# Receptance product moved ahead of the value product and the numerator scan in an RWKV block's time mix, on eight cores

## The chip, the cores and the metric

The kernel runs on all 8 cores of one Trainium2 chip, each core with one of the 8 sequences of the batch and its own copy of all weights. The cores exchange nothing. The metric is the device time in microseconds (us) of the slowest core; lower is better.

## The reference, cut to what matters

One RWKV layer (time mix, then channel mix) with a residual and a layer norm around it, then a feed-forward layer with dequantized weights and again a residual and a layer norm. Each core has 4096 rows of 1024 values. The change lies in the time mix:

```python
xn = _ln(x, ln1_g, ln1_b)
xp = _shift(xn)
k = (xn * mix_k + xp * (1.0 - mix_k)) @ Wk
v = (xn * mix_v + xp * (1.0 - mix_v)) @ Wv
r = jax.nn.sigmoid((xn * mix_r + xp * (1.0 - mix_r)) @ Wr)
# _wkv, over the positions t:
#   ek = exp(k_t);  a = ew * a + ek * v_t;  b = ew * b + ek
#   out_t = a / (b + 1e-8)
wkv = _wkv(k, v, time_decay, time_first)
x = x + r * wkv @ Wo
```

The two recurrences have one decay `ew` for each feature. The quotient is computed as `a * exp(-ln(b + 1e-8))`.

## The kernel before, in words

A core works through its rows in 8 blocks of 512 positions (h = 0 to 7). The Python code records all instructions once, in program order, with the buffers that each reads and writes; every engine then runs its own instructions in that order, and a semaphore wait is put in wherever another engine (or the same one, where a result is needed at once) must be done first. Nothing is reordered, so the order in which the code records is the order of the work. Buffers are tracked by name: `T1` and `T2` are one name each, though they hold 8 slices of 512 columns, while the 32 slices of `bigbf` have a name each (`bg0` to `bg31`).

For a block the stages are: load and first layer norm (`stage_pre`), transposes (`stage_tr1`), the mixes (`stage_mix_k`, and `stage_mix_vr`, which makes all 8 slices for v and then all 8 for r on VectorE), `stage_attn`, the channel mix (`stage_fA`), the middle norm, the feed-forward (`stage_fB`), and the last norm (`stage_tail`). `stage_pre` of the next block is recorded inside `stage_fA`, `stage_mix_k` inside `stage_fB`. `stage_mix_vr` and `stage_attn` stand alone between one block's tail and its own `stage_fA`.

`stage_attn` has these parts, each over 8 output slices `mo` of 128 features; a product of one slice is 8 matmuls of 512 columns into one PSUM bank (`kvr_mm`, L614):

1. k loop: k product, then ScalarE takes the exponential into `T1` (L633).
2. v loop: v product into the four banks psA, psB, psO0, psO1 in turn; VectorE multiplies it with `T1` into `sc_ekv` (L651); ScalarE writes the decay into one of two halves of `ew_t` (L657); VectorE scans the numerator (L662), copies the carry (L668), scans the denominator (L673), copies that carry (L679); ScalarE takes Ln (L682) and Exp (L686); VectorE multiplies both into `T2` (L690).
3. r loop: r product into the two banks psO2 and psO3; ScalarE takes the sigmoid into the single buffer `rsg` (L706); VectorE multiplies it with `T2` into a slice of `bigbf` (L709).
4. Wo part: four groups j of 16 matmuls (L733 into psO0 or psO2, L739 into psO1 or psO3), after each of which VectorE adds the residual (L747), forms a second sum (L751) and the row sums of the second layer norm (L498), and ScalarE the squares (L507). The norm ends with Ln and Exp on ScalarE (L517, L520).

The weights of the four products stream through three buffers `wsm0` to `wsm2`, each of which holds half a matrix (1 MB), by DMAs that SyncE issues in program order. In block 0 the weights must first be cast to bf16: `pump_pair` records two jobs, each a load, a cast on ScalarE or VectorE, and a store. Block 0 records two pairs in each turn of the k loop, one in each turn of the v loop, two in each turn of the r loop and one in each group of the Wo part. Every core of the eight does all of this for itself.

Of the kernel before, what the change touches and what calls it, by code (L numbers as in the profile page):

```python
# [167 lines left out]
def build_program():  # L168
# [54 lines left out]
    with contextlib.ExitStack() as st:  # L223
# [398 lines left out]
        def stage_attn(h):  # L622
# [21 lines left out]
            E("q_sync", lambda e: e.dma_start(out=wsm[0][:], in_=s_wv[1]),  # L644
              reads=["s_wv@0", "s_wv@1"], writes=["wsm0"], tag=f"{hh}_ldv1")
            E("q_sync", lambda e: e.dma_start(out=wsm[1][:], in_=s_wr[0]),
              reads=["s_wr@0", "s_wr@1"], writes=["wsm1"], tag=f"{hh}_ldr0")
            for mo in range(KT):
                ps, psn = kvr_mm(hh, mo, wsm[2], "wsm2", wsm[0], "wsm0", 8,
                                 f"{hh}_vmm")  # L650
                E("vector", lambda e, mo=mo, ps=ps: e.tensor_tensor(  # L651
                    out=sc_ekv[:], in0=T1[:, 512 * mo:512 * (mo + 1)], in1=ps[:],
                    op=OP.mult),
                  reads=["T1", psn], writes=["ekv"], tag=f"{hh}_ekv{mo}")
# [7 lines left out]
                E("vector", lambda e, mo=mo, ese=ese: e.tensor_tensor_scan(  # L662
                    out=sc_aa[:], data0=ew_t[:, ese],
                    data1=sc_ekv[:], initial=vca[:, mo:mo + 1],
                    op0=OP.mult, op1=OP.add),
                  reads=[f"ewt{sl_e}", "ekv"], sreads=["vca"], writes=["aa"],
                  tag=f"{hh}_sa{mo}")
                E("vector", lambda e, mo=mo: e.tensor_copy(  # L668
                    out=vca[:, mo:mo + 1], in_=sc_aa[:, 511:512]),
                  sreads=["aa"], writes=["vca"], tag=f"{hh}_ca{mo}")  # L670
# [19 lines left out]
                E("vector", lambda e, mo=mo, bo=bo: e.tensor_tensor(  # L690
                    out=T2[:, 512 * mo:512 * (mo + 1)], in0=sc_aa[:],
                    in1=sc_bb[:, bo:bo + 512], op=OP.mult),
                  reads=["aa", bn], writes=["T2"], tag=f"{hh}_wk{mo}")
                if h == 0:
                    pump_pair("scalar", "scalar")
            E("q_sync", lambda e: e.dma_start(out=wsm[2][:], in_=s_wr[1]),
              reads=["s_wr@0", "s_wr@1"], writes=["wsm2"], tag=f"{hh}_ldr1")
            E("q_sync", lambda e: e.dma_start(out=wsm[0][:], in_=s_wo[0]),
              reads=["s_wo@0", "s_wo@1"], writes=["wsm0"], tag=f"{hh}_ldo0")
            sig_fns = []  # L700
            for mo in range(KT):
                ps, psn = kvr_mm(hh, mo, wsm[1], "wsm1", wsm[2], "wsm2", 16,
                                 f"{hh}_rmm", pool=RPS)

                def mkf(mo=mo, ps=ps, psn=psn):
                    E("scalar", lambda e: e.activation(  # L706
                        out=rsg[:], in_=ps[:], func=AF.Sigmoid),
                      reads=[psn], writes=["rsg"], tag=f"{hh}_sg{mo}")
                    E("vector", lambda e: e.tensor_tensor(  # L709
                        out=bigbf[:, 512 * (24 + mo):512 * (25 + mo)],  # L710
                        in0=rsg[:], in1=T2[:, 512 * mo:512 * (mo + 1)],
                        op=OP.mult),
                      reads=["rsg", "T2"], writes=[bbuf(24 + mo)],
                      tag=f"{hh}_gt{mo}")
                sig_fns.append(mkf)
                if mo > 0:
                    sig_fns[mo - 1]()
# [319 lines left out]
```

How the kernel before makes its waits and increments, by code:

```python
        def run_stream(eng_name, eng):  # L150
            for it in items:
                if DMA_QUEUES.get(it["stream"], it["stream"]) != eng_name:
                    continue
                for s, v in sorted(it["waits"].items()):
                    eng.wait_ge(sems[s], v)
                inst = it["fn"](eng)
                if it["signals"]:
                    step = 16 if it["stream"] in DMA_QUEUES else 1
                    assert inst is not None, f"item {it['idx']} {it['tag']}"
                    inst.then_inc(sems[it["skey"]], step)
```

## Time and profile before

| what | us |
|---|---|
| median of the two timed runs | 4782.44 |
| those two runs | 4756.19 and 4808.68 |
| the profiled execution's own time | 4536.96 |
| its span on the slowest core (core 7) | 4535.4 |
| spans of the eight cores | 4494.7 to 4535.4 |

The span is the time from the first to the last instruction of a core. The profiled execution is the one from which all rows below are read; its own time is 1.6 us above its span. Each row of the timeline names its start, its length, the engine, the line of the kernel before, the operation, and what it writes and reads; where the engine stood idle before it, the idle time and the releaser stand in brackets.

### The profile page before, as it was taken

What the parts mean: (1) busy time and instruction counts of PE and PEld (TensorE: products, weight loads), DVE (VectorE), ACT (ScalarE), POOL (GpSimd) and SP (SyncE); (2) the same over time, 40 slices, a digit from 0 to 9 for tenths busy, and PEclk for the clock granted to TensorE, in tenths of its full rate; (3) what the DMA queues carried; (4) which work ended last, traced back from release to release, by engine and by line L of the source; (5) the groups of instructions that cost most, each with busy time, mean ns of one, the idle gap of its engine ahead of it and who ended that gap; (6) DMA issues with size and microseconds to landing.
All of it is one profiled execution on the core that took longest, in us unless ns stands there. A gap on an engine that the chain in (4) does not pass through costs nothing.

```text
span 4535.4 us, 41048 instructions; the slowest of 8 cores (4494.7 to 4535.4 us)
## 1 busy us (share of the span) xinstructions
PE 2980.6 (66%) x11840; PEld 1207.2 (27%) x11840; DVE 1480.0 (33%) x2843; ACT 1086.0 (24%) x1670; POOL 170.2 (4%) x292
## 2 busy tenths in 40 slices
PE   1121269978658765878476956786587658784966
PEld 0000022323223322333132312332233223331422
DVE  2321233431641155213622163215411552136121
ACT  1121132213131313222232123121313132212221
POOL 2112201210000000000000000000000000000000
PEclk9555666678879887989788968897798879896988
DMA  6555445543323331434132412333233314341323
GB/s 151 155 168 185 158 142 175 190 132 111 106 81 114 105 118 54 128 90 137 69 107 84 135 73 102 100 114 110 74 118 107 112 54 130 95 149 54 107 93 109
DMA packets 260843, 521.08 MB, mean 115 GB/s; under 512 B 26081, under 2 KB 81633, under 8 KB 250386
## 3 DMA queue, kind: packets, MB, share of 16 engines
q1 hardware_dynamic: 178096, 387.52, 26.7%
q0 software_dynamic: 24192, 79.28, 5.3%
q10 hardware_dynamic: 58338, 51.66, 3.9%
q8 instruction: 103, 1.69, 0.2%
q14 instruction: 114, 0.93, 0.1%
HBM read 457.54 MB, written 60.82 MB: 114 GB/s over the span
## 4 chain that ended last, share of the span: by engine, by line
PE 42%; DMA 22%; DVE 19%; ACT 8%; issue 7%; DVEq 1%; POOL 1%; ACTq 1%; SPq 0%; POOLq 0%
PE psO L809 14%; PE psA L841 9%; PE psB L841 8%; DMA fvb<-s_w 4%; DMA fvb<-s_fv 3%; DVE bigbf L581 2%; DVE stB_sum L498 2%; DMA s_fv<-stb 2%; DVE sc_bb L572 2%; DMA s_w<-stb 2%; PE psO L614 2%; DVE sc_aa L662 2%; DMA stf<-L_attn_Wfk 2%; DVE sc_bb L673 2%; DMA fkb<-s_w 1%
## 5 line engine op out<-in xcount | busy, mean ns | idle before, releaser
L809 PE MATMUL psO<-fvb,bigbf 128*128 128x512 bf16 x4096 | 1076.8, 399 | 219.5 <-DMA fvb<-s_w 71.3
L809 PEld LDWEIGHTS psO<-fvb,bigbf 128*128 128x128 bf16 x4096 | 394.0, 101 | 843.4 <-issue 462.1
L614 PE MATMUL psO<-bigbf,wsm 128*128 128x512 bf16 x1024 | 296.5, 455 | 379.9 <-ACT rsg L706 253.9
L841 PE MATMUL psB<-TB,fkb 128*128 128x512 bf16 x2048 | 518.2, 399 | 39.6 <-DMA fkb<-s_fk 34.2
L841 PE MATMUL psA<-TB,fkb 128*128 128x512 bf16 x2048 | 513.5, 396 | 16.0 <-DMA fkb<-s_fk 8.5
L867 DVE TENSOR_TENSOR bigbf<-bigbf 128x512 bf16<-128x512 bf16 x256 | 108.4, 425 | 685.3 <-ACT bigbf L863 685.3
L934 DVE SCALAR_TENSOR_TENSOR T<-Q,psO 128x512 f32<-128x512 f32 x64 | 44.0, 688 | 864.1 <-PE psO L927 859.1
L545 PE MATMUL psT<-ident_sb,ztm 128*128 128x128 bf16 x512 | 69.5, 292 | 344.9 <-DVE ztm L524 205.4
L614 PE MATMUL psA<-bigbf,wsm 128*128 128x512 bf16 x256 | 100.9, 522 | 291.4 <-DVE sc_ekv L651 88.6
L841 PEld LDWEIGHTS psB<-TB,fkb 128*128 128x128 bf16 x2048 | 206.6, 102 | 320.5 <-issue 117.0
L841 PEld LDWEIGHTS psA<-TB,fkb 128*128 128x128 bf16 x2048 | 204.7, 102 | 290.0 <-issue 81.7
L507 ACT ACTIVATE zt<-T,stB_nm 128x1024 bf16<-128x1024 f32 x64 | 73.6, 1151 | 854.4 <-DVE stB_m L504 854.4
L614 PEld LDWEIGHTS psO<-bigbf,wsm 128*128 128x128 bf16 x1024 | 111.9, 112 | 566.4 <-issue 488.9
L682 ACT ACTIVATE sc_bb<-sc_bb,ce 128x512 f32<-128x512 f32 x64 | 46.3, 723 | 457.4 <-DVE vcb L679 457.4
L344 ACT ACTIVATE stb<-stf 128x1024 bf16<-128x1024 f32 x60 | 62.7, 1055 | 374.7 <-DMA s_fv<-stb 70.2
L863 ACT ACTIVATE bigbf<-psB 128x512 bf16<-128x512 f32 x128 | 76.4, 597 | 307.1 <-PE psB L841 283.9
L919 ACT ACTIVATE bigbf<-psA,vfb 128x512 bf16<-128x512 f32 x128 | 88.2, 689 | 241.2 <-PE psA L841 241.1
L733 PE MATMUL psO<-wsm,bigbf 128*128 128x512 bf16 x256 | 103.0, 402 | 64.0 <-DMA wsm<-s_wo 43.7
L919 ACT ACTIVATE bigbf<-psB,vfb 128x512 bf16<-128x512 f32 x128 | 88.2, 689 | 234.0 <-PE psB L841 234.0
L876 DVE TENSOR_TENSOR sc_ekv<-T,psO 128x512 f32<-128x512 f32 x64 | 44.0, 688 | 304.0 <-PE psO L809 301.2
L545 PEld LDWEIGHTS psT<-ident_sb,ztm 128*128 128x128 bf16 x512 | 44.0, 124 | 372.5 <-issue 370.8
L863 ACT ACTIVATE bigbf<-psA 128x512 bf16<-128x512 f32 x128 | 76.5, 598 | 272.6 <-PE psA L841 228.8
(136 smaller groups left out, 2993.3 us busy)
## 6 DMA issues: line engine op xcount, KB each, us to landing
fkb<-s_fk SPq DMA_DIRECT2D x256, 256.0 KB, 2.8
fvb<-s_fv SPq DMA_DIRECT2D x256, 256.0 KB, 2.7
fkb<-s_w SPq DMA_DIRECT2D x256, 256.0 KB, 2.8
fvb<-s_w SPq DMA_DIRECT2D x256, 256.0 KB, 2.8
stq<-L_ffn_fc_q ACTq DMA_DIRECT2D x128, 256.0 KB, 4.4
x<-xcore SPq DMA_DIRECT2D x8, 2048.0 KB, 9.6
wsm<-s_wk SPq DMA_DIRECT2D x16, 1024.0 KB, 7.0
wsm<-s_wv SPq DMA_DIRECT2D x16, 1024.0 KB, 8.8
```

Of the source, the lines that this page charges most:

```text
L498: E("vector", lambda e, j=j: e.reduce_sum(out=ssum[:, j:j + 1], in_=srcten[:, 1024 * j:1024 * (j + 1)], axis=AX.X), reads=[srcbuf], writes ...
L545: E("tensor", lambda e, ci=ci, j=j, pst=pst: e.transpose(pst[:, 128 * j:128 * (j + 1)], srcten[:, 1024 * j + 128 * ci:1024 * j + 128 * (ci ...
L572: E("vector", lambda e, ci=ci: e.tensor_tensor(out=sc_bb[:, 1:512], in0=TA[:, 512 * ci + 1:512 * (ci + 1)], in1=TA[:, 512 * ci:512 * (ci + ...
L581: E("vector", lambda e, ci=ci, vm=vm: e.scalar_tensor_tensor(out=bigbf[:, 512 * (slot + ci) + 1:512 * (slot + ci + 1)], in0=sc_bb[:, 1:512 ...
L614: E("tensor", lambda e, mo=mo, k=k, ps=ps, wt=wt: e.matmul(ps[:], wt[:, 1024 * (k % 4) + 128 * mo:1024 * (k % 4) + 128 * (mo + 1)], bigbf[ ...
L662: E("vector", lambda e, mo=mo, ese=ese: e.tensor_tensor_scan(out=sc_aa[:], data0=ew_t[:, ese], data1=sc_ekv[:], initial=vca[:, mo:mo + 1], ...
L733: E("tensor", lambda e, p0=p0, wt=wt, k=k, gsl=gsl: e.matmul(p0[:], bigbf[:, gsl], wt[:, 1024 * (k % 4):1024 * (k % 4) + 512], start=(k == ...
L809: E("tensor", lambda e, mm=mm, j=j, mpar=mpar, sl=sl: e.matmul(psO[j][:], bigbf[:, 512 * mm + 128 * j:512 * mm + 128 * (j + 1)], fvb[:, 10 ...
L841: E("tensor", lambda e, m=m, k=k, ps=ps, par=par: e.matmul(ps[:], fkb[:, 1024 * par + 128 * k:1024 * par + 128 * (k + 1)], TB[:, 512 * k:5 ...
L863: E("scalar", lambda e, ps=ps, m=m: e.activation(out=bigbf[:, 512 * m:512 * (m + 1)], in_=ps[:], func=AF.Relu), reads=[psn], writes=[bbuf( ...
L867: E("vector", lambda e, m=m: e.tensor_tensor(out=bigbf[:, 512 * m:512 * (m + 1)], in0=bigbf[:, 512 * m:512 * (m + 1)], in1=bigbf[:, 512 * ...
L919: E("scalar", lambda e, m=m, ps=ps: e.activation(out=bigbf[:, 512 * m:512 * (m + 1)], in_=ps[:], func=AF.Silu, bias=vfb1[:, m:m + 1]), rea ...
```

## The change

The r loop now comes before the v loop, and the work of the old v loop is divided between the two.

- New r loop: r product, the sigmoid straight into the slice of `bigbf` (L650; `rsg` is gone), the decay (L656), the denominator scan and its carry (L663, L669), Ln and Exp, the latter into `T2` (L672, L676). Block 0 records its two pairs of casts here.
- New v loop: v product, the product with `T1` (L690), the decay once more (L696), the numerator scan and its carry (L701, L707), the product with `T2` in place (L710) and with the sigmoid in place (L714). Block 0 records its one pair here.
- The weight loads are exchanged accordingly, and in block 0 the casts of `Wr` come before those of `Wv`.

The core of the diff:

```diff
@@ r loop (new place) @@
+                ps, psn = kvr_mm(hh, mo, wsm[2], "wsm2", wsm[0], "wsm0", 16,
+                                 f"{hh}_rmm", pool=RPS)
+                E("scalar", lambda e, mo=mo, ps=ps: e.activation(
+                    out=bigbf[:, 512 * (24 + mo):512 * (25 + mo)], in_=ps[:],
+                    func=AF.Sigmoid),
+                  reads=[psn], writes=[bbuf(24 + mo)], tag=f"{hh}_sg{mo}")
...
-                E("scalar", lambda e, bo=bo: e.activation(
-                    out=sc_bb[:, bo:bo + 512], in_=sc_bb[:, bo:bo + 512],
-                    func=AF.Exp, scale=-1.0),
-                  sreads=[bn], writes=[bn], tag=f"{hh}_eb{mo}")
+                E("scalar", lambda e, mo=mo, bo=bo: e.activation(
+                    out=T2[:, 512 * mo:512 * (mo + 1)],
+                    in_=sc_bb[:, bo:bo + 512], func=AF.Exp, scale=-1.0),
+                  sreads=[bn], writes=["T2"], tag=f"{hh}_eb{mo}")
...
@@ v loop (new place) @@
+                ps, psn = kvr_mm(hh, mo, wsm[1], "wsm1", wsm[2], "wsm2", 8,
+                                 f"{hh}_vmm")
...
+                E("scalar", lambda e, mo=mo, ese=ese: e.activation(
+                    out=ew_t[:, ese], in_=ew_t[:, ese], func=AF.Exp, scale=0.0,
+                    bias=vtd[:, mo:mo + 1]),
+                  reads=[f"ewt{sl_e}"], sreads=["vtd"], writes=[f"ewt{sl_e}"],
+                  tag=f"{hh}_ew2{mo}")
...
+                E("vector", lambda e, mo=mo: e.tensor_tensor(
+                    out=T2[:, 512 * mo:512 * (mo + 1)], in0=sc_aa[:],
+                    in1=T2[:, 512 * mo:512 * (mo + 1)], op=OP.mult),
+                  reads=["aa", "T2"], writes=["T2"], tag=f"{hh}_wk{mo}")
+                E("vector", lambda e, mo=mo: e.tensor_tensor(
+                    out=bigbf[:, 512 * (24 + mo):512 * (25 + mo)],
+                    in0=bigbf[:, 512 * (24 + mo):512 * (25 + mo)],
+                    in1=T2[:, 512 * mo:512 * (mo + 1)], op=OP.mult),
+                  reads=[bbuf(24 + mo), "T2"], writes=[bbuf(24 + mo)],
+                  tag=f"{hh}_gt{mo}")
```

ScalarE, block 1, from the last two turns of the old v loop into the old r loop (before):

```order
L657 ACTIVATE ew_t<-ew_t,vtd 128x512
L682 ACTIVATE sc_bb<-sc_bb,ce8 128x512
L686 ACTIVATE sc_bb<-sc_bb 128x512
L657 ACTIVATE ew_t<-ew_t,vtd 128x512
L682 ACTIVATE sc_bb<-sc_bb,ce8 128x512
L686 ACTIVATE sc_bb<-sc_bb 128x512
L706 ACTIVATE rsg<-psO2 128x512
L706 ACTIVATE rsg<-psO3 128x512
```

The same engine and block after the change, the last two turns of the new r loop and the whole new v loop, up to the second layer norm:

```order
L650 ACTIVATE bigbf<-psO2 128x512
L656 ACTIVATE ew_t<-ew_t,vtd 128x512
L672 ACTIVATE sc_bb<-sc_bb,ce8 128x512
L676 ACTIVATE T2<-sc_bb 128x512
L650 ACTIVATE bigbf<-psO3 128x512
L656 ACTIVATE ew_t<-ew_t,vtd 128x512
L672 ACTIVATE sc_bb<-sc_bb,ce8 128x512
L676 ACTIVATE T2<-sc_bb 128x512
L696 ACTIVATE ew_t<-ew_t,vtd 128x512 x8
L506 ACTIVATE ztm,stB_vs<-Q,stB_nm 128x1024 x4
L516 ACTIVATE stB_rs<-stB_vs,ce5 128x4
```

The sigmoids (L706, now L650) stood in one run of eight behind all Exp and Ln; now each stands between the Exp of one turn and the Exp of the next. Eight decays (L696) are new.

VectorE, block 1, one turn of the old v loop and the start of the next (before):

```order
L651 TENSOR_TENSOR sc_ekv<-T,psA 128x512
L662 SCALAR_TENSOR_TENSOR sc_aa<-ew_t,vca,sc_ekv 128x512
L668 COPY vca<-sc_aa 128x1
L673 SCALAR_TENSOR_TENSOR sc_bb<-ew_t,vcb,T 128x512
L679 COPY vcb<-sc_bb 128x1
L690 TENSOR_TENSOR T<-sc_aa,sc_bb 128x512
L651 TENSOR_TENSOR sc_ekv<-T,psB 128x512
```

VectorE, block 1, after the change, the last turn of the new r loop, the first turn of the new v loop and the start of its second:

```order
L663 SCALAR_TENSOR_TENSOR sc_bb<-ew_t,vcb,T 128x512
L669 COPY vcb<-sc_bb 128x1
L690 TENSOR_TENSOR sc_ekv<-T,psA 128x512
L701 SCALAR_TENSOR_TENSOR sc_aa<-ew_t,vca,sc_ekv 128x512
L707 COPY vca<-sc_aa 128x1
L710 TENSOR_TENSOR T<-sc_aa,T 128x512
L714 TENSOR_TENSOR bigbf<-bigbf,T 128x512
L690 TENSOR_TENSOR sc_ekv<-T,psB 128x512
```

The denominator scan left the turn of the numerator, and both products stand in that turn now, the sigmoid's (L709, now L714) among them.

TensorE, the last two products and the first matmuls of the Wo part (before):

```order
L614 MATMUL psO2<-bigbf,wsm1 128x512 x4
L614 MATMUL psO2<-bigbf,wsm2 128x512 x4
L614 MATMUL psO3<-bigbf,wsm1 128x512 x4
L614 MATMUL psO3<-bigbf,wsm2 128x512 x4
L733 MATMUL psO0<-wsm0,bigbf 128x512
L739 MATMUL psO1<-wsm0,bigbf 128x512
```

The same place after the change:

```order
L613 MATMUL psO0<-bigbf,wsm1 128x512 x4
L613 MATMUL psO0<-bigbf,wsm2 128x512 x4
L613 MATMUL psO1<-bigbf,wsm1 128x512 x4
L613 MATMUL psO1<-bigbf,wsm2 128x512 x4
L733 MATMUL psO0<-wsm0,bigbf 128x512
L739 MATMUL psO1<-wsm0,bigbf 128x512
```

The Wo part now starts in the two banks that the last two v products leave behind; before, it started in two that the r products did not use.

## Rows read from the trace of the kernel before

**Rows 1.** The page, DMA issues: what, queue, count, KB each, us to landing.

```profile
wsm<-s_wv SPq DMA_DIRECT2D x16, 1024.0 KB, 8.8
```

**Rows 2.** Groups by line: busy us, mean ns | idle before, releaser.

```profile
L690 DVE TENSOR_TENSOR T<-sc_aa,sc_bb 128x512 f32<-128x512 f32 x64 | 44.3, 693 | 105.4 <-ACT sc_bb L686 105.4
```

**Rows 3.** Timeline, one turn of block 7's v loop: start us, us, engine, line.

```profile
4117.15 0.68 DVE L651 TENSOR_TENSOR sc_ekv<-T,psO 128x512 f32<-128x512 f32 x1
4117.93 1.29 DVE L662 TENSOR_TENSOR_SCAN sc_aa<-ew_t,vca,sc_ekv 128x512 f32<-128x512 f32 x1
4119.32 0.15 DVE L668 COPY vca<-sc_aa 128x1 f32<-128x1 f32 x1
4119.39 1.27 DVE L673 TENSOR_TENSOR_SCAN sc_bb<-ew_t,vcb,T 128x512 f32<-128x512 f32 x1
4120.77 0.15 DVE L679 COPY vcb<-sc_bb 128x1 f32<-128x1 f32 x1
4121.02 0.72 ACT L682 ACTIVATE sc_bb<-sc_bb,ce 128x512 f32<-128x512 f32 x1 [3.97 <-DVE vcb L679]
4121.83 0.63 ACT L686 ACTIVATE sc_bb<-sc_bb 128x512 f32<-128x512 f32 x1
4122.37 0.71 ACT L657 ACTIVATE ew_t<-ew_t,vtd 128x512 f32<-128x512 f32 x1
4122.57 0.69 DVE L690 TENSOR_TENSOR T<-sc_aa,sc_bb 128x512 f32<-128x512 f32 x1 [1.64 <-ACT sc_bb L686]
4123.18 0.68 DVE L651 TENSOR_TENSOR sc_ekv<-T,psO 128x512 f32<-128x512 f32 x1
```

**Rows 4.** Timeline, block 7: end of the v loop, r loop, Wo part, second norm.

```profile
4151.97 0.63 ACT L686 ACTIVATE sc_bb<-sc_bb 128x512 f32<-128x512 f32 x1
4152.61 1.28 ACT L706 ACT_TABLE_LOAD   x1
4153.91 0.60 ACT L706 ACTIVATE rsg<-psO 128x512 bf16<-128x512 f32 x1
4154.65 13.32 PE L614 MATMUL psO<-bigbf,wsm 128*128 128x512 bf16 x48 [20.88 <-ACT rsg L706]
...
4172.31 0.38 PE L733 MATMUL psO<-wsm,bigbf 128*128 128x512 bf16 x1 [2.61 <-DMA wsm<-s_wo]
...
4174.09 0.69 DVE L747 TENSOR_TENSOR Q<-x,psO 128x512 f32<-128x512 f32 x1 [4.57 <-PE psO L733]
...
4195.52 1.28 ACT L517 ACT_TABLE_LOAD   x1
```

**Rows 5.** What line 706, line 517 and line 316 ran, with the counts.

```profile
L706 ACT ACT_TABLE_LOAD  x8: 1283/1283/1283, 382.7 to 4152.6; - x8
...
L517 ACT ACT_TABLE_LOAD  x23: 1283/1283/1283, 577.0 to 4521.0; - x23
...
L316 ACT ACT_TABLE_LOAD  x1: 1283/1283/1283, 30.2 to 30.2; - x1
```

**Rows 6.** Timeline, block 7: end of the mixes, and a matmul behind a mix.

```profile
4084.09 0.59 PE L614 MATMUL psA<-bigbf,wsm 128*128 128x512 bf16 x1 [1.66 <-DVE bigbf L588]
4104.31 0.22 DVE L588 SCALAR_TENSOR_TENSOR bigbf<-sc_bb,vmr,vcx 128x1 bf16<-128x1 f32 x1
...
4104.80 0.69 DVE L651 TENSOR_TENSOR sc_ekv<-T,psA 128x512 f32<-128x512 f32 x1
```

**Rows 7.** Stretches of block 7: length, busy us of PE, PEld, DVE, ACT, POOL, clock, DMA.

```profile
4154.60:4158.00 3.40, 3.35 (x8) 1.16 (x9) 1.39 (x2) 0.60 (x1) 0.00 (x0) 0.50 0.00 0
4158.00:4162.00 4.00, 4.00 (x15) 1.58 (x14) 0.77 (x2) 1.20 (x2) 0.00 (x0) 0.71 0.00 0
4162.00:4168.00 6.00, 6.00 (x29) 2.73 (x28) 2.69 (x4) 1.79 (x3) 0.00 (x0) 1.00 0.00 0
```

**Rows 8.** Stretches of block 0: old v loop, and old r loop.

```profile
280.00:360.00 80.00, 19.72 (x48) 6.14 (x48) 31.46 (x47) 29.21 (x37) 13.66 (x22) 0.61 0.58 181
...
384.00:530.00 146.00, 25.61 (x62) 7.70 (x62) 13.70 (x21) 18.77 (x22) 31.91 (x59) 0.56 0.51 166
```

More of the change, by code:

```diff
@@ L236, in build_program @@
         sc_bb = T("sc_bb", [128, 1024], F32)
-        rsg = T("rsg", [128, 512], BF16)
         wsm = [T(f"wsm{i}", [128, 4096], BF16) for i in range(3)]
@@ L359, in cast_job @@
             cast_jobs.append((emit_in, emit_rest))
-        for wname, whbm, scr in [("s_wk", Wk, s_wk), ("s_wv", Wv, s_wv),
-                                 ("s_wr", Wr, s_wr), ("s_wo", Wo, s_wo),
+        for wname, whbm, scr in [("s_wk", Wk, s_wk), ("s_wr", Wr, s_wr),
+                                 ("s_wv", Wv, s_wv), ("s_wo", Wo, s_wo),
                                  ("s_wfr", Wfr, s_wfr)]:
@@ L627, in stage_attn @@
               reads=["s_wk@0", "s_wk@1"], writes=["wsm1"], tag=f"{hh}_ldk1")
-            E("q_sync", lambda e: e.dma_start(out=wsm[2][:], in_=s_wv[0]),
-              reads=["s_wv@0", "s_wv@1"], writes=["wsm2"], tag=f"{hh}_ldv0")
+            E("q_sync", lambda e: e.dma_start(out=wsm[2][:], in_=s_wr[0]),
+              reads=["s_wr@0", "s_wr@1"], writes=["wsm2"], tag=f"{hh}_ldr0")
             for mo in range(KT):
@@ L643, in stage_attn @@
                     pump_pair()
[L644 to L647, printed above, removed]
+            E("q_sync", lambda e: e.dma_start(out=wsm[0][:], in_=s_wr[1]),
+              reads=["s_wr@0", "s_wr@1"], writes=["wsm0"], tag=f"{hh}_ldr1")
+            E("q_sync", lambda e: e.dma_start(out=wsm[1][:], in_=s_wv[0]),
+              reads=["s_wv@0", "s_wv@1"], writes=["wsm1"], tag=f"{hh}_ldv0")
             for mo in range(KT):
[L649 to L654, printed above, removed]
+                ps, psn = kvr_mm(hh, mo, wsm[2], "wsm2", wsm[0], "wsm0", 16,
[4 more added lines that the diff above has]
+                  reads=[psn], writes=[bbuf(24 + mo)], tag=f"{hh}_sg{mo}")
                 sl_e = mo % 2
@@ L661, in stage_attn @@
                   tag=f"{hh}_ew{mo}")
[L662 to L670, printed above, removed]
                 bo = 512 * (mo % 2)
@@ L685, in stage_attn @@
                   sreads=[bn, "ce8"], writes=[bn], tag=f"{hh}_lb{mo}")
-                E("scalar", lambda e, bo=bo: e.activation(
-                    out=sc_bb[:, bo:bo + 512], in_=sc_bb[:, bo:bo + 512],
-                    func=AF.Exp, scale=-1.0),
-                  sreads=[bn], writes=[bn], tag=f"{hh}_eb{mo}")
[L690 to L717, printed above, removed]
+                E("scalar", lambda e, mo=mo, bo=bo: e.activation(
+                    out=T2[:, 512 * mo:512 * (mo + 1)],
+                    in_=sc_bb[:, bo:bo + 512], func=AF.Exp, scale=-1.0),
+                  sreads=[bn], writes=["T2"], tag=f"{hh}_eb{mo}")
                 if h == 0:
@@ L720, in stage_attn @@
                     pump_pair()
-            sig_fns[KT - 1]()
+            E("q_sync", lambda e: e.dma_start(out=wsm[2][:], in_=s_wv[1]),
+              reads=["s_wv@0", "s_wv@1"], writes=["wsm2"], tag=f"{hh}_ldv1")
+            E("q_sync", lambda e: e.dma_start(out=wsm[0][:], in_=s_wo[0]),
+              reads=["s_wo@0", "s_wo@1"], writes=["wsm0"], tag=f"{hh}_ldo0")
+            for mo in range(KT):
+                ps, psn = kvr_mm(hh, mo, wsm[1], "wsm1", wsm[2], "wsm2", 8,
+                                 f"{hh}_vmm")
+                E("vector", lambda e, mo=mo, ps=ps: e.tensor_tensor(
+                    out=sc_ekv[:], in0=T1[:, 512 * mo:512 * (mo + 1)], in1=ps[:],
+                    op=OP.mult),
+                  reads=["T1", psn], writes=["ekv"], tag=f"{hh}_ekv{mo}")
+                sl_e = mo % 2
+                ese = slice(512 * sl_e, 512 * (sl_e + 1))
+                E("scalar", lambda e, mo=mo, ese=ese: e.activation(
[3 more added lines that the diff above has]
+                  tag=f"{hh}_ew2{mo}")
+                E("vector", lambda e, mo=mo, ese=ese: e.tensor_tensor_scan(
+                    out=sc_aa[:], data0=ew_t[:, ese],
+                    data1=sc_ekv[:], initial=vca[:, mo:mo + 1],
+                    op0=OP.mult, op1=OP.add),
+                  reads=[f"ewt{sl_e}", "ekv"], sreads=["vca"], writes=["aa"],
+                  tag=f"{hh}_sa{mo}")
+                E("vector", lambda e, mo=mo: e.tensor_copy(
+                    out=vca[:, mo:mo + 1], in_=sc_aa[:, 511:512]),
+                  sreads=["aa"], writes=["vca"], tag=f"{hh}_ca{mo}")
+                E("vector", lambda e, mo=mo: e.tensor_tensor(
[8 more added lines that the diff above has]
+                  tag=f"{hh}_gt{mo}")
+                if h == 0:
+                    pump_pair("scalar", "scalar")
```

## The prediction

> **What bounds the kernel now.** I read the head of the page first, then the groups by line, then the timeline of block 7, and last the counts of single lines. The slowest core spans 4535.4 us. `stage_attn` lies in no other stage's shadow: its v loop is a chain over two engines. In the groups the product L690 waited for ScalarE in 64 turns, 105.4 us together, 1.65 us in each [rows 2], so every block is alike there. The timeline shows one turn: VectorE does L651, both scans and both carries one behind the other, ScalarE starts Ln 0.25 us after the last carry, then Exp, and only then may VectorE multiply and begin the next turn [rows 3]. From one L651 to the next it is 4123.18 - 4117.15 = 6.03 us. The r loop follows and adds a short stretch: the sigmoid needs a table load of 1.28 us, TensorE waited 20.88 us for that sigmoid, and then runs 48 matmuls in 13.32 us [rows 4]. From the first L651 at 4104.80 [rows 6] to the first residual sum L747 at 4174.09 [rows 4] it is 69.3 us. This stretch is what the change rebuilds, and whatever it gains or loses goes into the span once for each block, since TensorE has nothing else to do there.
>
> **The change, part by part.** I rebuild block 7 from the same starting point, the end of the last r mix at 4104.53 [rows 6]. The mixes themselves are unchanged.
>
> *Table loads.* ScalarE loaded a table only when the function changed between Sigmoid and the pair Exp and Ln: 8 loads before L706, one for each block, though each block has 8 sigmoids [rows 5]. An Exp and a Ln that follow each other need one load together: the load at 30.2 served an Exp, and the first load in front of a Ln at L517 comes only at 577.0, after the first sigmoids, though the first layer norm took its Ln long before [rows 5]. In the new r loop a sigmoid stands behind an Exp, and a decay (Exp) behind the sigmoid. So each turn has 2 loads, 16 in a block where there were 2 (before L706 and before L517 of the second norm). The one at L517 goes, since eight decays now come last. Net 14 more in a block, 112 in all. None can hide: in this loop ScalarE's own instructions are the chain, and the load stands in line behind the Exp. Its cost from row to row: Exp starts at 4151.97, load at 4152.61 (0.64), sigmoid at 4153.91 (1.30) [rows 4].
>
> The page "ScalarE: Activation LUTs" of the Trainium skill, section "Table sets: the hidden batching unit", says to batch activations by set and not by function, which speaks against this change; the trace's 8 loads for 64 sigmoids agree.
>
> *One turn of the new r loop*, all of it serial, as nothing in it is double. Ln to Exp 0.81, Exp to load 0.64, load to sigmoid 1.30 [rows 3, 4]; sigmoid (0.60 long) to the second load 0.61, load to decay 1.30 [rows 4]; decay 0.71 long, and 0.11 to VectorE as from Exp to L690, 0.82; scan to carry 1.38, carry to Ln 0.25 [rows 3]. Sum 7.11 us. The r product is hidden: 8 matmuls take 3.4 us at the lower clock [rows 7], and two banks are there. Could it be less? The scan must wait for the decay and the decay for the sigmoid ahead of it in ScalarE's queue, so no. This term has narrow bounds, 7.0 to 7.3.
>
> *Start.* The r product needs the last r mix: 4104.53 + 0.14 + 0.59 for a matmul behind a mix, then 0.10 to ScalarE: 4105.4 [rows 6]. Load, sigmoid, load, decay, scan, carry put the first carry at 4110.8. The eighth is at 4110.77 + 7 x 7.11 = 4160.5. What is queued behind on VectorE is only the v loop; before, it began 55.8 us earlier.
>
> *Hand-over.* The first v multiply starts at 4160.6. Its scan needs the new decay L696, which stands behind the last Ln and Exp on ScalarE: Ln 4160.8, Exp 4161.6, decay 4162.1, scan 4163.0, a wait of 1.5 us on VectorE that did not exist. The later seven decays run ahead in ScalarE's idle time, up to the two halves of `ew_t`. L710 also needs the last Exp, long done by 4164.4.
>
> *One turn of the new v loop*, VectorE alone: multiply to scan 0.78, scan to carry 1.39, to the next 0.07 [rows 3], product L710 and then L714 which needs it, 0.78 (as L651 to L662), and 0.61 to the next turn (as L690 to L651). Sum 3.63. First turn's L714 at 4165.2, eighth multiply at 4165.8 + 6 x 3.63 = 4187.6, eighth L714 done at 4191.3. The v products are hidden, since four banks can be filled in the r loop: `wsm2` comes free after the last r product, which is released by the sixth sigmoid, some 18 us before the v loop, and a load of half a matrix takes 8.8 us [rows 1]. If this cover went, the price would be one load, under 9 us a block.
>
> *Wo part.* Its first matmul into psO1 must now wait for the eighth multiply L690, done at 4188.3. TensorE has stood still before, so it starts at the lower level: after a stand of 20.88 us it ran 8 matmuls in 3.4 us at clock 0.50 (1.2 GHz), reached the upper one (2.4 GHz) within the next stretch at 0.71, about 5.7 us from its start, and then did 29 in 6 us [rows 4, 7]. Thirteen matmuls at 0.43 put the last of psO0 at 4194.0, done at 4194.4, L747 at 4194.5. At the upper level throughout it would be gated by L714 and be 4191.9, which is the lower bound. The wait for `wsm1` of 2.61 us [rows 4] is gone, as that load is issued in the middle of the v loop.
>
> *Sum of a block.* 4194.5 - 4174.1 = +20.4, less the load at L517, 1.28 [rows 4]: +19.1 us; bounds +16.5 and +21. Seen by parts: 8 turns of 6.03 and the r loop of 21 go, 8 of 7.11 and 8 of 3.63 come, with 12 around them. Blocks 1 to 7: 7 x 19.1 = 134.
>
> *Block 0.* Its loops run at the pace of the casts: 80 us for 8 turns with one pair each, and 146 for 8 with two [rows 8], while ScalarE is busy 29 and 19 us of these. The count of pairs is unchanged. ScalarE's chain of 7.11 us in a turn of 18 fits, but holds up casts behind it; the new v loop frees it. I take +3; bounds -10 (the v loop's turns drop to the pace of the r loop's) and +25 (a table load pair in each turn fully added).
>
> Together +137 us on the profiled execution: 4536.96 + 137 = 4674, +3.0%. The median of the runs shown is 5.4% above the profiled execution. The added time lies on ScalarE and VectorE, so I add the same 137 to the median: 4782.44 + 137 = 4919.
>
> **Rivals.**
>
> *A, the loads don't appear or overlap a wait (not slower).* The place is ScalarE in the r loop. Without them a turn is 7.11 - 2.61 = 4.50 us, a block is 18 to 21 us cheaper, so -2 to +1, and the whole is 4770 to 4790. It decides once 5 of the 14 extra loads of a block fail to cost, which brings a block under 13 us and the whole under 2%. For it: the loop halves VectorE's wait for Ln and Exp. Against it: where a function changed, the load stood in line, with ScalarE idle neither before nor behind it [rows 4].
>
> *B, three loads in a turn.* If Exp behind a sigmoid fetches a table without Ln, Ln needs its own: 8 x 1.3 = 10.4 us more in a block, 29.5 instead of 19.1, 7 x 29.5 + 3 = 210, time 4992. For it: in this trace no Exp follows a sigmoid directly. Against: the Exp at L316 was served by a load that also served the first Ln [rows 5].
>
> *C, each change of table drains the engine as well.* With a stall of the load's own length, 14 x 1.3 = 18 us more in a block: 37, time 5045. Against: the load started 0.01 us after the Exp had ended, and the sigmoid 0.02 after the load [rows 4].
>
> The page "ScalarE: Activation LUTs", section "What ACT_TABLE_LOAD costs", gives 1283 ns and a drain of about 1380 ns on top, 2.66 us for a switch; by that rule the estimate is rival C's. The trace agrees with the 1283 and shows no room for the drain.
>
> *D, the clock.* If TensorE stays at the upper level through the v loop, a block costs 16.5: 7 x 16.5 + 3 = 118, time 4901. It lies in the forecast's own range.
>
> **How the numbers follow.** The forecast (D and the bounds of block 0 included) gets 0.84, A 0.06, B 0.06, C 0.04. The forecast's own range is 4885 to 4960: 7 x 16.5 - 10 = 105 and 7 x 21 + 25 = 172, rounded outward at the top for the spread of the runs shown. The range given is wider. The top, 4990, stops just short of B. The low end reaches over A down to the sum on the profiled execution's own scale, 4674, because two runs shown and the profiled execution stand 5% apart and I cannot tell on which the changed kernel will be timed. About 2% is what a measurement of this kernel can tell from no change. Slower by over 2% is the forecast, B and C, less some for block sums under 13 us: 0.90. Within 2% is A and that rest, 0.08. Faster 0.02.
>
> **What would show it.** In the changed kernel's groups: 64 table loads before L650 and 64 before L656, none before L672, and L516 with 8 fewer. From sigmoid to sigmoid 7.1 us in blocks 1 to 7, from multiply to multiply 3.6, a wait of about 1.5 us before the first numerator scan, and TensorE at clock 0.50 at the start of the Wo part. From the last r mix to the first L747 some 90 us where there were 69.6. If a turn of the r loop took 4.5 us, A is right; 8.4, B; 9.7 or more, C. I am wrong if the block's stretch grows by less than 13 us, or if block 0 moves by more than 25.

## The result, and the profile after

| | kernel before | changed kernel |
|---|---|---|
| median, us | 4575.37 (10 runs) | 4671.16 (12 runs) |
| fastest run, us | 4522.56 | 4651.57 |
| profiled execution, us | 4536.96 | 4651.57 |
| span of the slowest core, us | 4535.4 | 4650.0 |
| ratio to the kernel before | 1 | 1.028, 95% interval 1.0253 to 1.0307 |

The changed kernel is slower by 2.8%. In the experiments below every run of the kernel before over 4600 us had a core with a granted clock of 0.787 or less, while the others had 0.795 or more on every core, and the two timed runs ahead of the prediction, 4756.19 and 4808.68, were most likely of the first kind; the medians in the table hold such runs of both kernels, and the ratio, like every ratio below, leaves them out.

The head of the page of the changed kernel, core 6:

```profile
span 4650.0 us, 41167 instructions; the slowest of 8 cores (4616.5 to 4650.0 us)
...
PE 3023.7 (65%) x11840; PEld 1209.4 (26%) x11840; DVE 1479.7 (32%) x2843; ACT 1278.9 (28%) x1846; POOL 169.5 (4%) x292
```

TensorE and VectorE run as many instructions as before. ScalarE has 193 us more to do (1086.0 before), and 112 of its new instructions are table loads. The groups by line of the same kernel (busy us, mean ns | idle before, releaser):

```profile
L650 ACT ACT_TABLE_LOAD x64 | 82.1, 1283 | 220.8 <-PE psO L613 219.8
L656 ACT ACT_TABLE_LOAD x64 | 82.1, 1283 | 1.1
L663 DVE TENSOR_TENSOR_SCAN sc_bb<-ew_t,vcb,T 128x512 f32<-128x512 f32 x64 | 82.2, 1284 | 340.4 <-ACT ew_t L656 340.4
L701 DVE TENSOR_TENSOR_SCAN sc_aa<-ew_t,vca,sc_ekv 128x512 f32<-128x512 f32 x64 | 82.2, 1284 | 78.4 <-ACT ew_t L696 72.9 <-DVE sc_ekv L690 0.5
...
L516 ACT ACT_TABLE_LOAD x15 | 19.2, 1283 | 1.1
```

There are 64 loads before the sigmoid and 64 before the decay; L516, which was L517, has 8 fewer than in [rows 5]. In the kernel before VectorE waited 105.4 us for Ln and Exp [rows 2]. Now the denominator scan waits 340.4 us for the decay, behind both loads. That is the new bound of the r loop. One turn of it in block 7, on ScalarE (start us, us):

```profile
4240.00 0.72 ACT L672 ACTIVATE sc_bb<-sc_bb,ce 128x512 f32<-128x512 f32 x1 [1.81 <-DVE vcb L669]
4240.81 0.63 ACT L676 ACTIVATE T<-sc_bb 128x512 f32<-128x512 f32 x1
4241.46 1.28 ACT L650 ACT_TABLE_LOAD   x1
4242.75 0.60 ACT L650 ACTIVATE bigbf<-psO 128x512 bf16<-128x512 f32 x1
4243.37 1.28 ACT L656 ACT_TABLE_LOAD   x1
4244.66 0.72 ACT L656 ACTIVATE ew_t<-ew_t,vtd 128x512 f32<-128x512 f32 x1
4247.19 0.72 ACT L672 ACTIVATE sc_bb<-sc_bb,ce 128x512 f32<-128x512 f32 x1 [1.81 <-DVE vcb L669]
```

From Ln to Ln it is 7.19 us; ScalarE is idle only for the 1.81 us in which VectorE scans. The hand-over to the v loop and its first turn, on VectorE and, in the second row, ScalarE:

```profile
4261.43 0.69 DVE L690 TENSOR_TENSOR sc_ekv<-T,psA 128x512 f32<-128x512 f32 x1
...
4262.93 1.32 ACT L696 ACTIVATE ew_t<-ew_t,vtd 128x512 f32<-128x512 f32 x2
...
4263.80 1.28 DVE L701 TENSOR_TENSOR_SCAN sc_aa<-ew_t,vca,sc_ekv 128x512 f32<-128x512 f32 x1 [1.68 <-ACT ew_t L696]
...
4266.05 0.69 DVE L714 TENSOR_TENSOR bigbf<-bigbf,T 128x512 bf16<-128x512 bf16 x1
4266.66 0.68 DVE L690 TENSOR_TENSOR sc_ekv<-T,psB 128x512 f32<-128x512 f32 x1
```

The scan waits 1.68 us for the first of the new decays. The following turns, of which none waits, take 3.63 us. And the start of the Wo part:

```profile
4289.31 0.59 PE L739 MATMUL psO<-wsm,bigbf 128*128 128x512 bf16 x1 [3.05 <-DVE sc_ekv L690]
...
4291.51 0.69 DVE L714 TENSOR_TENSOR bigbf<-bigbf,T 128x512 bf16<-128x512 bf16 x1
...
4295.51 0.69 DVE L747 TENSOR_TENSOR Q<-x,psO 128x512 f32<-128x512 f32 x1 [3.31 <-PE psO L733]
```

```profile
4290.00:4295.00 5.00, 5.00 (x13) 1.82 (x12) 2.00 (x4) 0.00 (x0) 0.00 (x0) 0.50 0.00 0
```

The last row has the columns of [rows 7]. TensorE waits for the eighth multiply and then does its first matmuls at clock 0.50 (1.2 GHz), 13 in 5 us, so the first residual sum comes 3.3 us after the last gate.

From the end of the last r mix (L587, 4204.19 + 0.22) to this L747 it is 91.1 us. The median of this stretch is 90.3 (each core's median over blocks 1 to 7, and then the median of the eight cores, here and below). In the kernel before it was 4174.09 - 4104.53 = 69.6 in the same block [rows 4, 6], 69.2 in the median. The experiments below are compared by this stretch, since it is free of what happens elsewhere. What lies between one L747 and the next last r mix has not changed: about 408 us before and 407 after.

### The profile page after: what moved, and what is told of

Read it like the earlier page. It is cut to its first block, busy times and chain, and to the rows that moved or that the text cites. A ratio compares the mean times of both kernels' runs of the same rounds, so it can differ in the third digit from the quotient of the medians.

```text
span 4650.0 us, 41167 instructions; the slowest of 8 cores (4616.5 to 4650.0 us)
## 1 busy us (share of the span) xinstructions
PE 3023.7 (65%) x11840; PEld 1209.4 (26%) x11840; DVE 1479.7 (32%) x2843; ACT 1278.9 (28%) x1846; POOL 169.5 (4%) x292
## 4 chain that ended last, share of the span: by engine, by line
PE 39%; DMA 20%; DVE 19%; ACT 11%; issue 8%; DVEq 1%; POOL 1%; ACTq 0%; SPq 0%; POOLq 0%
PE psO L809 14%; PE psA L841 9%; PE psB L841 8%; DMA fvb<-s_w 3%; DMA fvb<-s_fv 3%; DVE bigbf L580 2%; DMA s_w<-stb 2%; DVE stB_sum L497 2%; DVE sc_bb L571 2%; DMA s_fv<-stb 2%; ACT L650 2%; DVE sc_bb L663 2%; ACT L656 2%; DMA stf<-L_attn_Wfk 1%; DVE sc_aa L701 1%
## 5 line engine op out<-in xcount | busy, mean ns | idle before, releaser
L809 PE MATMUL psO<-fvb,bigbf 128*128 128x512 bf16 x4096 | 1075.3, 397 | 219.7 <-DMA fvb<-s_w 67.8
L613 PE MATMUL psO<-bigbf,wsm 128*128 128x512 bf16 x1024 | 344.6, 494 | 537.2 <-ACT bigbf L650 218.2
L663 DVE TENSOR_TENSOR_SCAN sc_bb<-ew_t,vcb,T 128x512 f32<-128x512 f32 x64 | 82.2, 1284 | 340.4 <-ACT ew_t L656 340.4
L613 PE MATMUL psA<-bigbf,wsm 128*128 128x512 bf16 x256 | 91.3, 505 | 151.1 <-DMA wsm<-s_wv 59.9
L343 ACT ACTIVATE stb<-stf 128x1024 bf16<-128x1024 f32 x60 | 63.1, 1055 | 358.3 <-DMA stf<-L_attn_Wfv 65.1
L650 ACT ACT_TABLE_LOAD x64 | 82.1, 1283 | 220.8 <-PE psO L613 219.8
```

The source lines that it names most:

```text
L613: E("tensor", lambda e, mo=mo, k=k, ps=ps, wt=wt: e.matmul(ps[:], wt[:, 1024 * (k % 4) + 128 * mo:1024 * (k % 4) + 128 * (mo + 1)], bigbf[ ...
L650: E("scalar", lambda e, mo=mo, ps=ps: e.activation(out=bigbf[:, 512 * (24 + mo):512 * (25 + mo)], in_=ps[:], func=AF.Sigmoid), reads=[psn] ...
L663: E("vector", lambda e, mo=mo, ese=ese, bo=bo: e.tensor_tensor_scan(out=sc_bb[:, bo:bo + 512], data0=ew_t[:, ese], data1=T1[:, 512 * mo:51 ...
L809: E("tensor", lambda e, mm=mm, j=j, mpar=mpar, sl=sl: e.matmul(psO[j][:], bigbf[:, 512 * mm + 128 * j:512 * mm + 128 * (j + 1)], fvb[:, 10 ...
```

## The experiments

### The loads taken away

```diff
-                    func=AF.Sigmoid),
+                    func=AF.Exp),
                   reads=[psn], writes=[bbuf(24 + mo)], tag=f"{hh}_sg{mo}")
```

> The changed kernel with the sigmoid of the r loop replaced by Exp on the same operands (the gate is therefore exp(r), not sigmoid(r)), so no table change is left in the loop. My theory (the 14 extra table loads of a block carry the loss): a turn of the r loop falls from 7.2 to 4.6 us, the stretch from the last r mix to the first L747 from 90.2 to about 69 to 70 us, as in the kernel before, and the time comes to 4530 to 4550 us, ratio to before 0.995 +- 0.004. Rival (the loss is the split itself, the second decay, the hand-over and TensorE's cold start, with loads partly beside other work): the stretch stays above 80 us, ratio above 1.01.

The stretch was 67.8 us in the median. The two runs that count took 4495.09 and 4501.29 us, beside a median of 4533.8 of the kernel before on the same chip. On ScalarE (start us, us):

```profile
4087.84 0.72 ACT L672 ACTIVATE sc_bb<-sc_bb,ce 128x512 f32<-128x512 f32 x1 [1.81 <-DVE vcb L669]
4088.65 0.63 ACT L676 ACTIVATE T<-sc_bb 128x512 f32<-128x512 f32 x1
4089.18 0.58 ACT L650 ACTIVATE bigbf<-psO 128x512 bf16<-128x512 f32 x1
4089.66 0.71 ACT L656 ACTIVATE ew_t<-ew_t,vtd 128x512 f32<-128x512 f32 x1
4092.18 0.72 ACT L672 ACTIVATE sc_bb<-sc_bb,ce 128x512 f32<-128x512 f32 x1 [1.81 <-DVE vcb L669]
```

A turn takes 4.34 us instead of 7.19, so 2.85 for two loads and not 2.57. Most of the rest is overlap: without a load between them, one activation starts 0.09 to 0.10 us before the one ahead of it ends (4089.18 against 4088.65 + 0.63), twice in a turn. All of the loss is here, and a little more: 90.3 - 67.8 = 22.5 us a block. Without the loads the new order is better than the old one.

### The sigmoids in one run

```diff
-                    func=AF.Sigmoid),
-                  reads=[psn], writes=[bbuf(24 + mo)], tag=f"{hh}_sg{mo}")
+                    func=AF.Copy),
+                  reads=[psn], writes=[bbuf(24 + mo)], tag=f"{hh}_rc{mo}")
...
+            for mo in range(KT):
+                E("scalar", lambda e, mo=mo: e.activation(
+                    out=bigbf[:, 512 * (24 + mo):512 * (25 + mo)],
+                    in_=bigbf[:, 512 * (24 + mo):512 * (25 + mo)],
+                    func=AF.Sigmoid),
```

> The changed kernel with the r product copied to bf16 in its turn (Copy, no table of its own) and the eight sigmoids in place, in one run behind the r loop: 2 table loads a block instead of 16, but 8 more passes of 0.5 to 0.6 us on ScalarE. Table-load theory: a turn of the r loop 4.6 us, eight sigmoids and one load between the loops 6 us, one load before the decay of the v loop 1.3 us; part of this run delays the first decay of the v loop, so the stretch is 76 to 79 us, the time about 4585 us, ratio 1.005 to 1.015. Rival (the split itself): above 84 us, ratio above 1.02.

Ratio 1.0024, interval 1.0009 to 1.0039; stretch 74.8 us. This keeps every part of the change but the place of the sigmoids, and adds eight passes:

```profile
4148.16 1.28 ACT L684 ACT_TABLE_LOAD   x1
4149.45 4.26 ACT L684 ACTIVATE bigbf<-bigbf 128x512 bf16<-128x512 bf16 x8
4153.73 1.28 ACT L703 ACT_TABLE_LOAD   x1
```

Two loads and eight passes stand for 6.87 us between the loops, sixteen loads stood for 22.5. The stretch came out 1.2 us under the lowest value expected, but it is still 5.6 us longer than in the kernel before, so this batching takes the loss away and brings no gain. This is what the Trainium skill's page "ScalarE: Activation LUTs", section "Table sets: the hidden batching unit", asks for.

### Two more loads

```diff
+                if h > 0:
+                    E("scalar", lambda e: e.activation(
+                        out=rdum[:], in_=ce8[:], func=AF.Sigmoid),
+                      sreads=["ce8"], writes=["rdum"], tag=f"{hh}_dm{mo}")
```

> The changed kernel with one more sigmoid, of one column, between Ln and Exp in each turn of blocks 1 to 7: two more table loads a turn. If a load costs the chain its 1.28 us and nothing beyond, a turn grows by 2 x 1.29 + 0.3 = 2.9 us to 10.1, the stretch by 23 us to 113, the time by 7 x 23 = 162 us, ratio 1.064. If a change of table also drained the engine (a cost of 2.66 us for each), a turn would grow by 5.6 us, the time by 315 us, ratio 1.098. If loads overlapped waits, by less than 1.5 us a turn, ratio under 1.047.

The stretch was 111.8 us in the median and the profiled execution 4822.89, 1.063 of the 4536.96 of the kernel before; it is the only run that counts, so there is no interval. On ScalarE:

```profile
4394.55 0.63 ACT L681 ACTIVATE T<-sc_bb 128x512 f32<-128x512 f32 x1
...
4400.93 0.72 ACT L673 ACTIVATE sc_bb<-sc_bb,ce 128x512 f32<-128x512 f32 x1 [1.81 <-DVE vcb L670]
4401.67 1.28 ACT L678 ACT_TABLE_LOAD   x1
4402.97 0.20 ACT L678 ACTIVATE rdum<-ce 128x1 f32<-128x1 f32 x1
4403.19 1.28 ACT L681 ACT_TABLE_LOAD   x1
4404.48 0.63 ACT L681 ACTIVATE T<-sc_bb 128x512 f32<-128x512 f32 x1
```

A turn takes 9.93 us (from Exp to Exp), 2.74 more, the little activation included. A load costs its 1.28 us and 0.01 to 0.02 on either side. The drain of rival C would have made it 5.6 more; the 2.66 us for a switch that the Trainium skill's page "ScalarE: Activation LUTs" gives in its section "What ACT_TABLE_LOAD costs" do not hold in this place.

### The v products in other banks

```diff
+        VPS = [(psA, "psA"), (psB, "psB"), (psO[2], "psO2"), (psO[3], "psO3")]
...
-                                 f"{hh}_vmm")
+                                 f"{hh}_vmm", pool=VPS)
```

> The changed kernel with the v products in psA, psB, psO2, psO3 instead of psA, psB, psO0, psO1, so that the Wo part starts in banks that no v product holds. My step said that the Wo part's first matmuls wait for the eighth multiply and then run 13 matmuls at the lower clock, 2.6 us later than the last gate would allow. Theory: the first L747 comes 2 to 2.6 us earlier, stretch 87.6 to 88.2, 7 x 2.3 = 16 us less, ratio 1.024. Rival (TensorE is not what the first L747 waits for, or the group is gated by the last gate and the clock anyway): stretch 90, ratio 1.028.

The stretch was 88.6 us in nearly every block, 1.7 less. The expectation was 2 to 2.6. The ratio, 1.0284 with an interval of 1.0215 to 1.0354, can't tell 12 us in 4660 apart. The trace can:

```profile
4300.50 0.69 DVE L715 TENSOR_TENSOR bigbf<-bigbf,T 128x512 bf16<-128x512 bf16 x1
4301.34 0.58 PE L734 MATMUL psO<-wsm,bigbf 128*128 128x512 bf16 x1 [2.62 <-DVE bigbf L715]
...
4302.03 0.69 DVE L748 TENSOR_TENSOR Q<-x,psO 128x512 f32<-128x512 f32 x1 [0.84 <-PE psO L734]
```

TensorE now waits for the last gate and L748 follows 0.84 us behind it. The shared bank is a true wait of the change, and a small one.

### The decays not written at all

```diff
-                    out=sc_bb[:, bo:bo + 512], data0=ew_t[:, ese],
+                    out=sc_bb[:, bo:bo + 512], data0=vew[:, mo:mo + 1].to_broadcast([128, 512]),
```

The 16 decays of a block (L656, L696) go; `vew` holds exp of `vtd` and is computed once.

> The changed kernel without the decays written by ScalarE: both scans read exp of the decay from one column, broadcast, computed once. That takes 16 activations a block, makes the denominator scan free of ScalarE's queue and removes the hand-over wait of 1.7 us, but leaves 2 table loads in each turn (Sigmoid and Ln). Theory: loads stay on the chain, a turn is ScalarE alone: load, sigmoid, load, Ln, Exp, 4.7 us instead of 7.2; the stretch falls to 90.2 - 8 x 2.5 - 2 = 68 us, ratio about 0.992. Rival (a broadcast operand slows the scan, now 1.28 us, to more than 1.6): stretch over 72 us.

Ratio 0.9949, interval 0.9919 to 0.9979; stretch 67.8 us, as without the loads. The turn is 4.66 us and both loads are still in it:

```profile
4100.46 0.60 ACT L651 ACTIVATE bigbf<-psO 128x512 bf16<-128x512 f32 x1
4101.08 1.28 ACT L668 ACT_TABLE_LOAD   x1
4102.37 0.72 ACT L668 ACTIVATE sc_bb<-sc_bb,ce 128x512 f32<-128x512 f32 x1
4103.19 0.63 ACT L672 ACTIVATE T<-sc_bb 128x512 f32<-128x512 f32 x1
4103.83 1.28 ACT L651 ACT_TABLE_LOAD   x1
```

ScalarE is never idle here. The scan with the broadcast operand took 1.28 us as before, so the rival fell. The split pays once either the loads or the decays leave the chain.

### The sigmoid folded into the quotient

Since sigmoid(r) a / b = a exp(-ln((1 + exp(-r)) b)), the gate needs Exp and Ln only (the 1e-8 is now added to the whole product). On top of the broadcast decays:

```diff
-                    func=AF.Sigmoid),
+                    func=AF.Exp, scale=-1.0),
...
+                E("vector", lambda e, mo=mo, bo=bo: e.scalar_tensor_tensor(
+                    out=sc_bb[:, bo:bo + 512],
+                    in0=bigbf[:, 512 * (24 + mo):512 * (25 + mo)],
+                    scalar=1.0, in1=sc_bb[:, bo:bo + 512],
+                    op0=OP.add, op1=OP.mult),
...
-                    in0=bigbf[:, 512 * (24 + mo):512 * (25 + mo)],
-                    in1=T2[:, 512 * mo:512 * (mo + 1)], op=OP.mult),
```

> As the run with broadcast decays, and the sigmoid folded into the quotient: ScalarE takes exp(-r), VectorE multiplies (exp(-r) + 1) into the denominator ahead of Ln and Exp, and the last product of the v loop (the gate) goes. No table change in the loops at all. Theory: r loop 3.0 us a turn by ScalarE and VectorE but 3.6 where TensorE is at the lower clock, v loop 2.9 us a turn, the stretch 52 to 58 us against 69.3 before; less the load before the second norm, and block 0 some 12 us better: 7 x (-14 - 1.3) - 12 = about -120 us, 4420 us, ratio 0.972 to 0.980. Rival (TensorE or the hand-overs bind, no better than the split without loads): stretch 64 or more, ratio above 0.985.

Ratio 0.968, interval 0.9653 to 0.9707; stretch 50.8 us. ScalarE and VectorE in one turn of the r loop:

```profile
4001.05 0.69 DVE L668 SCALAR_TENSOR_TENSOR sc_bb<-bigbf,sc_bb 128x512 f32<-128x512 bf16 x1 [1.02 <-ACT bigbf L651]
4001.66 1.28 DVE L659 TENSOR_TENSOR_SCAN sc_bb<-vew,vcb,T 128x512 f32<-128x512 f32 x1
```

```profile
4001.84 0.72 ACT L675 ACTIVATE sc_bb<-sc_bb,ce 128x512 f32<-128x512 f32 x1 [0.96 <-DVE sc_bb L668]
4002.65 0.63 ACT L679 ACTIVATE T<-sc_bb 128x512 f32<-128x512 f32 x1
4003.19 0.58 ACT L651 ACTIVATE bigbf<-psO 128x512 bf16<-128x512 f32 x1
4004.73 0.72 ACT L675 ACTIVATE sc_bb<-sc_bb,ce 128x512 f32<-128x512 f32 x1 [0.96 <-DVE sc_bb L668]
```

The scan of the next turn now runs beside Ln and Exp, and a turn is 2.89 us; the v loop has 2.84. I had expected TensorE's lower clock to hold the r loop at 3.6; it did not: in the 25 us from 3985 to 4010 in block 7, which are this loop but for its ends, TensorE was busy 17.52 us and was granted 0.84. The gain was larger than the 0.972 to 0.980 that I had put down.

The same version with the v products in the other banks:

> The fused version (0.968 of the kernel before) with the v products in psA, psB, psO2, psO3, so that the Wo part's first banks are free. As in the changed kernel, where that took 1.6 us off the stretch: 50.5 to 48.5 or 49.5 us, 7 to 14 us in all, ratio 0.965 to 0.967; no change if the Wo part there is not held by the last multiply.

Ratio 0.9656, interval 0.9608 to 0.9704; stretch 48.0 us, 2.7 less before rounding, a little more than expected. The interval covers both, so the trace alone tells these two apart. Its cores had a granted clock of 0.776 to 0.794 in this trace and 0.818 to 0.825 in the other, so the 48.0 is not owed to a better clock.

### Block 0

The prediction's term for block 0 was +3 us. In the traces the stretch of block 0 went from 380.4 to 368.8 us (medians of the eight cores), and from its last r mix to that of block 1 it went from 1069.4 to 1061.2. The second figure is what counts for the time, and it scatters: the kernel with two more loads a turn in blocks 1 to 7 has the same block 0 as the changed kernel, and its trace gives 370.6 and 1070.7. So the shorter stretch is there in both traces, while the 8.1 us are less than two executions of one and the same block 0 differ by. Four runs were made for the cause. First, the kernel before with the last gate freed of the last casts:

```diff
                 if mo > 0:
                     sig_fns[mo - 1]()
+                if mo == KT - 1:
+                    sig_fns[mo]()
                 if h == 0:
                     pump_pair()
                     pump_pair()
-            sig_fns[KT - 1]()
```

> The kernel before with one edit for block 0: in the last turn of the old r loop the last sigmoid and gate are recorded ahead of that turn's two pairs of casts instead of behind them. Theory for block 0's gain of about 12 us (where I had forecast +3): in the kernel before, the last gate stands behind two pairs of casts in ScalarE's queue, in the changed kernel behind none of the last turn. Then the stretch of block 0 from its last r mix to its first L747 falls from about 380 us to 358 to 366, and the whole by 5 to 20 us, ratio 0.996 to 0.999. Rival (the gain came from the order of the cast jobs and their pace in the two loops): stretch stays at 375 to 385, ratio 1.000. Blocks 1 to 7 unchanged, 69.3.

Ratio 1.0011 (0.9991 to 1.0032), stretch 378.9 us, to the next block's mix 1069.5. My theory fell. The first residual sum (here L748) had been queued on VectorE behind the casts (L349) of the same pairs:

```profile
515.36 0.69 DVE L349 CAST stb<-stf 128x1024 bf16<-128x1024 f32 x1 [8.22 <-DMA s_fv<-stb]
515.97 0.68 DVE L748 TENSOR_TENSOR Q<-x,psO 128x512 f32<-128x512 f32 x1
```

Next, those casts all on ScalarE:

> As the earlier run on the last pairs (kernel before, block 0, last sigmoid and gate ahead of the last turn's two pairs), and in addition all four casts of these pairs on ScalarE. In that earlier run the first matmul group of the Wo part ended early, but the first L747 waited on VectorE behind the two casts of the last pairs. Theory: block 0's stretch depends on what stands ahead of the last gate and ahead of L747 on both engines, so with VectorE free of them it falls from 379 to 355 to 366 us; the four casts then delay the squares L507 on ScalarE, so the whole gains less, ratio 0.996 to 1.000. Rival (pace of the casts alone): 375 to 385 as in both kernels before it.

The stretch fell to 364.2 us as the theory had it, but the time to the next block's mix was 1073.0, no less than before, and the ratio 1.003 (0.9993 to 1.0067). So an earlier L747 in block 0 is worth nothing by itself that these runs can show. The likely reason is that the stage behind it waits for the casts, the last of which ended at 573.3 us from the start there and at 571.8 in the kernel before (medians of the cores). The opposite edit, in the changed kernel:

> The changed kernel with block 0's pair of casts in the v loop recorded at the head of each turn instead of its end, so that the last scan and gate stand behind one more pair: the opposite of the edit that freed the last gate. Theory: the stretch of block 0 grows from about 369 us by one pair, 6 to 11 us, to 375 to 380, time +0.1 to 0.25%. Rival (pace of the jobs alone): no change in it, 365 to 372. Blocks 1 to 7 unchanged at 90.2.

The stretch went to 376.5 us, and to 375.8 over cores 4 to 7, whose clock was 0.80 in this trace (0.77 on the others); this is again as the place of the last gate has it. The ratio was 1.0286 (1.0257 to 1.0316), no different from the changed kernel's.

What is left is the pace of the cast jobs. Here are the casts of 16 jobs (the ones that fell into the old v loop), on core 7, in the first row those of L344 on ScalarE and in the second those of L349 on VectorE: length of the stretch, busy us with the count, TensorE's clock, DMA share and GB/s. First the kernel before:

```profile
273.00:361.00 88.00, 15.31 (x15) 0.61 0.58 179
...
273.00:361.00 88.00, 0.69 (x1) 0.61 0.58 179
```

The same 16 in the changed kernel (L343 and L348), where they fall into the new r loop with two pairs a turn:

```profile
271.00:343.00 72.00, 8.46 (x8) 0.52 0.61 185
...
271.00:343.00 72.00, 5.55 (x8) 0.52 0.61 185
```

They take 72 us instead of 88. So the last run redistributed the pairs in the kernel before, and nothing else:

```diff
                 if h == 0:
-                    pump_pair("scalar", "scalar")
+                    pump_pair()
+                    pump_pair()
...
                 if h == 0:
-                    pump_pair()
-                    pump_pair()
+                    pump_pair("scalar", "scalar")
```

> The kernel before with only the casts of block 0 redistributed as the change does it in effect: two pairs in each turn of the (old) v loop and one pair, both casts on ScalarE, in each turn of the (old) r loop. In the traces the 16 jobs of the old v loop took 87 us, the same 16 in the new r loop 72, and the later ones 8 us more. Theory (block 0's gain of 12 us is the pace of the cast jobs: one pair in each turn of a 6 us chain runs slower than two): jobs 48 to 63 take 70 to 75 us, the last cast comes 5 to 12 us earlier, the last r mix of block 1 too, ratio 0.997 to 0.999. Rival (it came from the chain being another one): last cast within 3 us of before, ratio 1.000 +- 0.001.

```profile
273.00:345.00 72.00, 8.45 (x8) 0.57 0.61 185
...
273.00:345.00 72.00, 5.54 (x8) 0.57 0.61 185
```

The 16 jobs took 72 us here as well, behind the old chain, so the count of pairs in a turn set that pace and not the chain. But most of the 16 us did not last. From the end of these 16 jobs to the end of the last cast it was 208 us in the kernel before, 220 in the changed one and 222 here, and the last cast ended at 571.8, 563.5 and 568.3 us from the start (medians of the cores). So it came 3.5 us earlier in this run, less than the 5 to 12 that the theory asked for. The stretch of block 0 was 375.5 us, and to the next block's mix it was 1063.6, 5.7 less than before, which is also within what two executions of one block 0 differ by. Of the time only one run counts (4525.98), so there is no ratio. The faster pace of the 16 jobs is shown; that it brought the 8 us is not, nor that there were 8 us to bring.

## Why the prediction was right or wrong

**The time.** The forecast was 4919 us, and the measured median 4671, 3 us under the low end of 4674. What failed is the step "so I add the same 137 to the median: 4782.44 + 137 = 4919". The runs showed another base in its place: ten runs of the kernel before have a median of 4575.37, so 4782.44 - 4575.37 = 207 of the 248 us by which the forecast is too high lie in the base. The sum itself was made on the profiled execution and gave 4674 and +3.0%. That the measured median comes so near to it is partly luck, since +2.8% of 4537 is 127 us and not 137. Two runs that agree neither with each other (1.1% apart) nor with the profiled execution (5% below) were the weaker base. The direction and the chance for slower (0.90) were right.

**The number and place of the table loads.** Right: 128 in the loops, 8 fewer before the second norm, none hidden. Rival A fell by the 340.4 us that L663 waits for L656, B by the absence of a load before L672, C by a turn of 7.19 us and by the run with four loads, D by the clock of 0.50 at the start of the Wo part.

**The turn of the r loop.** 7.11 forecast, 7.19 measured. The whole difference lies between the decay and Ln, 2.45 forecast (0.82 + 1.38 + 0.25) and 2.53 measured (4247.19 - 4244.66). The price of a load was read as 1.30; taken away, it is 2.85 / 2 = 1.43, as activations that touch overlap by 0.09 to 0.10 us. So the forecast for rival A's world, "-2 to +1" against the kernel before, was too dear: without loads the stretch was 69.2 - 67.8 = 1.4 us shorter than before, and with the load at L516 gone the block gained 2.7.

**Start, hand-over, turn of the v loop.** Right: a wait of 1.5 us forecast for the second decay, 1.68 measured; 3.63 us a turn in both.

**The Wo part.** Right in kind: TensorE was held by the eighth multiply and ran 14 matmuls at the lower clock. Its price was too dear, 2.6 by the two bounds (19.1 - 16.5) and 1.7 by the run with other banks.

**Sum of a block.** The stretch was to grow by 20.4 and grew by 90.3 - 69.2 = 21.1; less the load before the second norm, 19.8 against 19.1. Times 7, 139 against 134.

**Block 0.** The step "I take +3; bounds -10" came out at -8 in this pair of traces and at +1 when the other trace with the changed block 0 is set against the kernel before (1070.7 - 1069.4). So the term was small, as taken, and its sign stays open. The reason given, "ScalarE's chain of 7.11 us in a turn of 18 fits, but holds up casts behind it", did not hold for the first 16 jobs: one pair in each turn of a 6 us chain had taken 88 us for them, and two pairs in each turn took 72, behind the new chain and behind the old one.

**Together.** 7 x 19.8 - 8 = 131 us on 4537, 2.9%, or 139 and 3.1% without a gain in block 0; the ratio says 2.8%, with an interval of 2.5 to 3.1.
